# Another order for the path sums, recurrences and shared experts beside the second alignment of a perceiver block

## What is computed

```python
# x (32, 64, 256), ctx (32, 1601, 256); per batch: dynamic time warping of ctx against layernorm(x)
D = sqrt(max(|small|^2 + |large|^2 - 2 small @ large.T, 0))        # 1601 x 64
R[i, j] = D[i, j] + min(R[i-1, j], R[i, j-1], R[i-1, j-1])          # way out
path = backtrack(R)                                                 # way back, from the last corner
x = x + zeros.at[j_of_path].add(ctx[i_of_path])                     # path sums: which rows of ctx go to which latent
# a recurrence over the 64 latents, after a layernorm h of x
r, k, v, w = sigmoid(h Wr'), h Wk', h Wv', 0.99 sigmoid(h Ww')
state = state * w + v k';  out = r * state.sum(-1);  x = x + rmsnorm(out) @ Wo'
# experts, after another layernorm h2: 2 of 8 routed (softmax, top 2), and one shared expert for every token
x = x + sum_e weight_e * ffn_e(h2) + ffn_shared(h2)                 # ffn = (silu(h w1') * (h w3')) w2'
```

## Time and profile before

| | |
|---|---|
| median of three runs | 1200.44 us |
| the profiled execution | 1200.08 us, of which 1198.8 us are its span |
| PE, DVE, ACT, POOL busy over the span | 990.3, 671.8, 489.1, 115.6 us |
| the chain that ended last | 56% PE, 28% DVE, 7% DMA |
| second alignment, way out | from 392 us to 569 us of the span |
| second alignment, way back, up to the second group's path terms | from 569 us to 682 us |
| in those 290 us: PE and DVE busy | 238.2 and 210.6 us |
| granted TensorE clock, way out and way back | 0.94 and 0.89 of full |

### The profile page before, as it was taken

How to read it: one execution, slowest core, us unless ns; L and a number is a source line. 1 busy time by engine, 2 the same in 40 slices (tenths; PEclk the granted TensorE clock), 3 DMA queues, 4 the chain that set the end, 5 groups by cost and what they waited for, 6 DMA issues and landing times.

```text
span 1198.8 us, 15398 instructions
## 1 busy us (share of the span) xinstructions
PE 990.3 (83%) x4836; PEld 590.1 (49%) x4836; DVE 671.8 (56%) x2330; ACT 489.1 (41%) x839; POOL 115.6 (10%) x150
## 2 busy tenths in 40 slices
PE   5886649888551699987897599888899999999998
PEld 2332213333220355553575365646676767676776
DVE  4994859999899677487669712435511111111116
ACT  4884626666661344423231255232222222222221
POOL 1000000000000000000000000000233434342210
PEclk9998979999876799998898799788899999999999
DMA  9999864447874979550050097394121212223115
GB/s 355 326 297 280 248 160 143 146 142 182 249 207 109 346 245 327 155 158 1 0 182 1 1 327 246 90 345 179 47 68 51 86 56 86 63 78 109 32 48 182
DMA packets 123663, 190.48 MB, mean 159 GB/s; under 512 B 8864, under 2 KB 92992, under 8 KB 123584
## 3 DMA queue, kind: packets, MB, share of 16 engines
q1 hardware_dynamic: 117696, 171.13, 46.7%
q0 software_dynamic: 5888, 18.36, 5.0%
HBM read 165.43 MB, written 24.03 MB: 158 GB/s over the span
## 4 chain that ended last, share of the span: by engine, by line
PE 56%; DVE 28%; DMA 7%; issue 3%; ACT 3%; SPq 2%; POOL 0%; DVEq 0%; ACTq 0%; POOLq 0%
PE bank L1753 13%; PE bank L1600 8%; PE bank L1784 7%; PE bank L1745 5%; PE bank L1621 5%; DVE table L790 4%; DMA spaced<-dist 3%; PE bank L1776 3%; PE bank L1764 3%; DVE passed L811 3%; DVE beyond L806 2%; DVE z L732 2%; DVE col_min L783 2%; DVE z L724 2%; PE bank L1544 2%
## 5 line engine op out<-in xcount | busy, mean ns | idle before, releaser
L992 DVE TENSOR_TENSOR hid<-bank,act_s 128x352 f32<-128x352 f32 x104 | 54.2, 524 | 229.2 <-PE bank L1753 182.3
L1753 PE MATMUL bank<-w_up,srcT 128*128 x512 | 162.8, 460 | 0.9 <-ACT srcT L1390 0.9
L1528 PE MATMUL bank<-sq,ones 128*64 128x402 f32 (+1 forms) x512 | 104.8, 532 | 43.9 <-ACT sq L1257 43.8
L1398 ACT ACTIVATE act_s<-bank 128x352 f32<-128x352 f32 x104 | 48.0, 463 | 202.0 <-PE bank L1753 127.9
L1522 PE MATMUL bank<-ctxT,latT 128*64 128x402 f32 (+1 forms) x512 | 104.7, 532 | 21.5 <-DMA ctxT<-ctx_tr_dram 20.8
L1544 PE MATMUL bank<-table,ident 128*128 128x402 f32 x144 | 67.1, 549 | 65.2 <-DVE stays L760 55.3
L1753 PEld LDWEIGHTS bank<-w_up,srcT 128*128 128x128 f32 x512 | 96.0, 189 | 48.1 <-issue 4.2
L1257 ACT ACTIVATE sq<-ctxT 128x1608 f32<-128x1608 f32 x64 | 97.5, 1526 | 15.8 <-DMA ctxT<-ctx_tr_dram 15.8
L1600 PE MATMUL bank<-rows_c,on_path 128*64 128x256 f32 (+1 forms) x832 | 98.3, 387 | 1.0 <-ACT on_path L1315 0.5
L1784 PE MATMUL bank<-w_dn,hidT 128*128 (+1 forms) x384 | 93.5, 380 | 0.4 <-DVE y_sb L1006 0.4
L1290 ACT ACTIVATE code<-bank,unpassed 128x402 bf16<-128x402 f32 x72 | 42.1, 590 | 123.6 <-PE bank L1546 123.6
(11 more groups left out here) (286 smaller groups left out, 1604.6 us busy)
## 6 DMA issues: line engine op xcount, KB each, us to landing
rows_c<-ctx_nat_dram SPq DMA_DIRECT2D x32, 896.0 KB
ctxT<-ctx_tr_dram SPq DMA_DIRECT2D x32, 804.0 KB, 8.6
ctxT<-ctx_tr_dram SPq DMA_DIRECT2D x32, 797.0 KB, 9.3
rows_c<-ctx_nat_dram SPq DMA_DIRECT2D x32, 640.0 KB
spaced<-dist SPq DMA_DIRECT2D x128, 101.0 KB, 5.0
w_up<-w_t_dram SPq DMA_DIRECT2D x16, 704.0 KB, 12.7
table<-spaced SPq DMA_DIRECT2D x16, 404.0 KB, 11.1
table<-spaced SPq DMA_DIRECT2D x32, 202.0 KB, 5.9
```

What stands on the lines that cost most here:

```text
L1528: last = e.matmul(ps[b * T:(b + 1) * T, 0:nq], ones[:, 0:T], sq[i][:, b, k, 0:nq], start=False, stop=(k == KC - 1))
L1753: last = e.matmul(psum[2 * i + m][:, 0:HH], srcT[t % 2][:, k, :], w_up[:, bass.ds(ex, 1), m, k, columns], start=(k == 0), stop=(k == KC - 1))
```

## The change

Two functions that say how many pieces follow a slot. There is one more line in the file, so all later line numbers are one higher after it.

```diff
 def behind_second(n):
     if n < 6:
         return 0
-    if n < 33:
-        return min((n - 6) % 4, 1)
     if n < CODE_SLOTS:
+
+        return (n + 1) % 2
+    if n < CODE_SLOTS + 18:
         return 1
-    if n < CODE_SLOTS + 21:
-        return min((n - CODE_SLOTS) % 3, 1)
-    return 1 if n % 4 == 0 else 0
+    if n < CODE_SLOTS + 60:
+        return 1 if n % 3 < 2 else 0
+    return 1 if n % 3 == 0 else 0
 
 def shared_beside(n):
-    return 1 if n >= 14 and n % 5 != 4 else 0
+    return 1 if n >= 2 and n % 5 in (0, 2) else 0
```

## The result

The changed kernel took 1222.05 us (median of four launches, 1212.02 to 1223.97) against 1200.62: ratio 1.0168, 95% interval 1.0121 to 1.0216. The sign was forecast, the size was not: 1208.8 was said, with a range up to 1219. Launched again beside other kernels it was at 1219.45 against 1198.93, ratio 1.0174 (1.0145 to 1.0203).

The account below looks back on a forecast made before the run. VectorE's fixed work plus waits was taken to bound the second alignment. Waits of 17.8 + 16.3 + 41.75 + 0.35 = 76.2 us against 67.5 gave 8.7 more than 1200.08, so 1208.8; own range 1203 to 1213, wider 1194 to 1219.

Parts of the forecast that it names:

- VectorE's waits set the stage: Second alignment, up to the second group's path terms: VectorE's work is fixed, only its waits change, from 67.5 to 76.2 us.
- Path sums and codes along the way out: Way out: VectorE's waits for path sums and gap products fall to 17.8 us, 3.1 less; two code waits come besides.
- Two earlier codes wait for ScalarE: Before the last codes: VectorE waits 2.3 and 1.1 us while ScalarE stands at a layernorm's square root.
- the turn: Between way out and way back: VectorE waits 12.9 us for the last codes; 16.3 with two earlier ones, against 4.3 before.
- The first pair's 3.9: Way out: the first block with both halves of a pair, entered with no head start, makes VectorE wait 3.9 us.
- the start's 1.3: Start of the way out: VectorE's wait there stays at 1.3 us.
- the 1.6, 1.0, 2.6 and 1.0: Way out: VectorE's waits in us, 1.6 beside a second half alone, the others beside two projections or a remaining half.
- Recurrences and shared experts: Way back: VectorE's waits for recurrence pieces and shared expert halves sum to 41.75 us, against 42.3 before.
- The halves' part: Way back: waits for shared expert halves, 11.75 + 7.65 = 19.4 us, bounds 0 and 46.
- The rival of halves that wait for nothing: Way back: TensorE and ScalarE run ahead of VectorE, so the 19.4 us vanish; 1189 us, chance 0.25.
- the rival of a lower clock: Way back: TensorE idles between pieces and returns at half clock, four more returns of 2.0 us; 1217 us, chance 0.16.
- Table loads: ScalarE: four loads on top of nine, 1.28 us each within waits already counted, each followed by its function at once.

Follow-up runs that it names:

- codes together: Changed kernel with ScalarE forming both halves of a block's move codes at one place of its list, after the third step; ratio 1.0014 to the kernel before.
- the kernel before with codes together: Kernel before the change, with only ScalarE's list edited so both halves of a block's codes stand at one place; ratio 0.9983 to the kernel before.
- the first order of 47 pieces: Changed kernel with both code halves at one place, 47 pieces on the way out, the rest at each second slot back; ratios 0.9951 and 0.9947 to before.

## Why the prediction was right in sign and wrong in size

**VectorE's waits set the stage: right.** The stage grew by 24.1 us, the waits by 22.7; VectorE's busy time was 1.4 longer. (In both kernels some 10.7 us of the stage are neither listed work nor listed wait.) Behind the stage nothing was lost (516.6 against 518.1). But the chain of waits was misread: in this stretch of the kernel before it runs mostly on TensorE, 189.5 us by the sum of its pieces, and on VectorE for 52.2. VectorE's waits are where TensorE's work shows, which fits that most other orders only moved them.

**Path sums and codes along the way out: the step that failed.** The prediction had `col_min` at 17.8 and "Two earlier codes wait for ScalarE" at 2.3 and 1.1, together 21.2. Measured: 6.1 and 27.4, together 33.5, 12.3 too many; the way out ended at 549.9 us instead of 538. I priced a pair's block by TensorE's own work, 10.0 against VectorE's 5.70, and let the wait end at `col_min`. I followed the order of ScalarE only at the turn, where the masks stand between two rows L1291 in the list that was printed ahead of the prediction. The same place is there along the whole way out, from the first mask on (the wait of 2.57 at 410.25), and the wait of 1.93 in the trace of before was a sign of it. With that place cleared the kernel does what the sum said: `col_min` 17.3 (17.8), the turn 12.1 (12.9), the way out 142.9 and the way back 153.4, where the forecast implied 146 (538 - 392) and 153. For the pairs this is not luck. Twice with codes together both halves and the two banks of gap products take TensorE 10.0 us (434.30 + 0.33 - 424.61, and from 457.00 to 467.02), as priced, and VectorE waits 3.16 and 3.15 behind them, where 3.2 was forecast:

```profile
424.61 3.24 PE L1601 MATMUL bank<-rows_c,on_path 128*64 128x256 f32 x28
...
434.30 0.33 PE L1547 MATMUL bank<-stays,tie 128*128 128x402 bf16 x1
```

```profile
434.67 0.37 DVE L784 TENSOR_TENSOR col_min<-table 128x201 f32<-128x201 f32 x1 [3.16 <-PE bank L1547]
```

The rest of `col_min` is in part luck. The first pair's 3.9 came as 3.76, but behind one half alone that had waited for a mask; the start's 1.3 as 1.57; and the 1.6, 1.0, 2.6 and 1.0 (6.2) as four waits of 0.29, 0.17, 4.37 and 0.81 (5.6).

Two slips in the sums are small: by its own numbers the first pair comes to 10.0 - 5.70 = 4.3, not 3.9, and two blocks less a step are 10.0, not 10.3.

**The turn: right.** 11.1 and 0.97 against 12.5 and 0.4, and ScalarE's last mask, from 545.37, stands ahead of the codes that end the 11.1, after 4.30 of idle for TensorE's products (L1579).

**Recurrences and shared experts: nearly right.** 41.75 was forecast, 44.6 measured (90.2 less 39.5 and 6.1). The halves' part, least known: 11.8 + 4.7 + 4.4 = 20.9 against 19.4; the recurrences' 23.7 against 22.35. The sign named was `hid` waits on TensorE near 20; these are 11.8, the rest waits for the SiLU and for down products. The rival of halves that wait for nothing is out.

**The clock: the rival's time, not its cause.** At 1217 the rival of a lower clock lies nearest to the result, and the way back's granted clock did fall, from 0.89 to 0.82:

```profile
549.90:707.20 157.30, 121.56 (x476) 86.37 (x476) 105.27 (x533) 43.33 (x68) 0.00 (x0) 0.82 0.20 65
```

(columns: window, length, busy time of PE, PEld, DVE, ACT and POOL with instructions, granted clock, DMA share, GB/s.) One return of the kind that was to decide is there: up products from 603.37 took 4.12 where dense ones take 2.53, and a `hid` waited 2.84 for them. That is 1.6 us, where four of 2.0 were supposed. The way back is only 3 to 4 us over the forecast, and with codes together it is 153.4 at a clock of 0.84, with the launch at 1201.0. What was missing was on the way out.

**Table loads: right.** There are 13 (4 and 9, before 3 and 6). As before, the function follows at once, and nothing stands idle ahead of the load:

```profile
593.27 0.20 ACT L1340 ACTIVATE ln_a<-ln_b 128x4 f32<-128x4 f32 x1 [7.66 <-DVE ln_b L681]
593.49 1.28 ACT L1399 ACT_TABLE_LOAD   x1
594.79 0.82 ACT L1399 ACTIVATE act_s<-bank 128x352 f32<-128x352 f32 x2
```

The Trainium skill (ScalarE: Activation LUTs, What ACT_TABLE_LOAD costs) gives about 1283 ns for the load itself, which the 1.28 here bears out, and about 1380 ns more for a drain, which these rows do not show; the measurement decides.

**The sum.** 1208.8 + 14.3 (waits of 90.2 against 75.9 of such groups) + 1.1 (busy time of 1.4 where 0.35 was set for the last addition) + 1.2 (the first path terms at 391.9 against 390.7) - 1.5 (behind the stage) = 1223.9; the profiled execution took 1223.97. These parts are measured, so the sum says where the time went and not why. The range failed with the forecast: it took its bounds from the halves' waits and the turn, and gave the codes along the way none.

## What to carry to other kernels

Where two lists are woven by slots, look in every engine's own list at what falls between the parts of one handover: a piece that waits for another engine, put between two halves of a result that are both ready, holds up whoever needs the whole. Thinning pieces out did not help here and their phase against the block did. Once no such place was left, every other distribution of the same work that was run gave waits of 66 to 75 us in a stage of 288 to 297, so a forecast of a mere redistribution should start near no change and look for the one blocking order.

## What the runs showed of the hardware

What follows the stage took 510.6 to 519.1 us in the fourteen profiles, a spread larger than what most orders changed, and one place goes with it: the output projection of the last recurrence, some 120 us behind the stage. In the kernel before, and in the kernel before with codes together, whose lists are the same there:

```profile
805.34 6.73 PE L1873 MATMUL bank<-w_o,kv 128*128 128x256 f32 x16 [2.93 <-DVE kv L1049]
```

```profile
803.10 3.69 PE L1873 MATMUL bank<-w_o,kv 128*128 128x256 f32 x16 [2.93 <-DVE kv L1049]
```

Each came after 2.93 us of idle and a stretch of projections at full clock (granted 1.00 from 792 to 802 us, and from 790 to 800). In the first the granted clock was then 0.54, in the second it stayed at 1.00; 518.1 and 512.8 us followed the stage. In all fourteen profiles the idle is 2.93 and the projection takes one of three lengths:

| length of the projection | profiles | what follows the stage |
|---|---|---|
| 3.69 | 5 | 510.6 to 513.2 |
| 5.15 to 5.38 | 6 | 513.7 to 517.3 |
| 6.69 to 6.73 | 3 | 518.1 to 519.1 |

What decides between them was not found out. The changed kernel (5.38 and 5.38) and the first order of 47 pieces (6.70 and 6.69) were profiled twice each and repeated theirs, so it is not shown that launches of one kernel differ at this place. It is why stages are compared above.
